# A two-layer graph kernel: 50 tiles of one class and 9 tiles of mixed classes in place of 73 padded tiles

## The reference, cut to what matters

```python
feat = concat([x[src], x[dst]], axis=1)            # 8192 x 2048
e = relu(feat[kind] @ W_kind + b_kind)             # 3 kinds: 128 hh, 640 oo, 7424 ho edges
logit = (e @ W_a + b_a)[:, 0]
alpha = softmax of logit over the edges with the same dst
z = segment_sum(alpha * x[src], dst)
new = relu(concat([x, z]) @ W_hn or W_on + b)      # nodes 0..63 and 64..255
x1 = layernorm(x + new)
```

## Time and profile before

| | us |
|---|---|
| median of three runs | 349.36 |
| span of the profiled execution, first to last instruction | 345.9 |
| what the median has beyond that span (start and end of an execution) | 3.5 |
| tile loop: first to last reduction on DVE | 142.3 to 229.2 |

### The profile page before, as it was taken

The page is one execution under the profiler, slowest core; times in us unless marked ns, Lnnn a source line. Parts: engine busy times, 40 slices in busy tenths (PEclk is TensorE's granted clock), DMA queues, the critical chain, the costliest instruction groups (busy, mean ns, idle before and its releaser), DMA issues.

```text
span 345.9 us, 4739 instructions
## 1 busy us (share of the span) xinstructions
PE 325.6 (94%) x1496; PEld 250.8 (73%) x1496; DVE 290.3 (84%) x415; ACT 195.6 (57%) x306; POOL 116.4 (34%) x128
## 2 busy tenths in 40 slices
PE   7899999999999999999999999999899999979980
PEld 7678887677644788588888888888686676758730
DVE  0999999973999979899999999988888877894545
ACT  3755396202043346588888888737149576821355
POOL 4200061084000840079999999720001200060000
PEclk9999999999999999999999999999999999999996
DMA  6999599789999996003030000023498886000003
GB/s 225 402 406 408 235 310 389 246 264 235 300 363 286 375 372 217 0 0 123 3 121 2 0 3 1 2 61 123 169 350 290 321 328 243 2 0 1 0 0 121
DMA packets 17654, 63.10 MB, mean 182 GB/s; under 512 B 2250, under 2 KB 2252, under 8 KB 17376
## 3 DMA queue, kind: packets, MB, share of 16 engines
q1 hardware_dynamic: 13536, 50.07, 39.1%
q0 software_dynamic: 2096, 8.74, 8.7%
q10 hardware_dynamic: 2000, 4.00, 3.5%
HBM read 59.64 MB, written 3.16 MB: 182 GB/s over the span
## 4 chain that ended last, share of the span: by engine, by line
DVE 45%; PE 43%; ACT 5%; DMA 2%; issue 2%; SPq 0%; ACTq 0%; DVEq 0%
DVE ps L1033 25%; PE ps L1227 12%; PE ps L1276 8%; DVE W_lo L796 5%; PE ps L1434 5%; PE ps L1505 4%; PE ps L1246 3%; DVE lo_in_raw L796 3%; PE ps L1442 2%; DMA W_raw<-in_L_gnn_W_oo_dram 2%; PE ps L1537 2%; PE ps L1469 2%; DVE tile_val L815 1%; PE ps L1308 1%; PE ps L1290 1%
## 5 line engine op out<-in xcount | busy, mean ns | idle before, releaser
L505 ACT CAST W_hi<-W_raw 128x1024 fp32r<-128x1024 f32 x62 | 63.0, 1045 | 58.6 <-DMA W_raw<-in_L_gnn_W_ho_dram 28.4
L1033 DVE SCALAR_TENSOR_TENSOR ps<-ps,wa_bc 128x1024 f32<-128x1024 f32 x73 | 86.4, 1261 | 1.3 <-PE ps L1392 1.3
L796 DVE TENSOR_TENSOR W_lo<-W_raw,W_hi 128x1024 fp32r<-128x1024 f32 x54 | 65.1, 1238 | 10.3 <-ACT W_hi L505 8.3
L1392 PE MATMUL ps<-A_tab,oh 128*128 x146 | 52.1, 438 | 0.8 <-DVE ps L1033 0.8
L1227 PE MATMUL ps<-W_hi,xT_hi 128*128 128x512 f32 x112 | 45.9, 410 | 1.0 <-DVE W_lo L796 0.9
L1392 PE MATMUL ps<-B_tab,oh 128*128 x146 | 45.9, 395 | 0.0
L1227 PE MATMUL ps<-W_lo,xT_hi 128*128 128x512 f32 x112 | 43.7, 390 | 0.0
L1227 PE MATMUL ps<-W_hi,xT_lo 128*128 128x512 f32 x112 | 34.6, 390 | 0.0
L454 POOL TENSOR_SCALAR sc<-sc 128x256 f32<-128x256 f32 x37 | 32.6, 882 | 3.2
L452 POOL TENSOR_TENSOR sc<-irow,keys 128x256 f32<-128x256 f32 x37 | 23.7, 641 | 26.5 <-PE ps L1399 26.0
L1392 PEld LDWEIGHTS ps<-B_tab,oh 128*128 128x128 f32 x146 | 27.4, 188 | 6.2 <-issue 0.5
(11 more groups left out here) (283 smaller groups left out, 585.4 us busy)
## 6 DMA issues: line engine op xcount, KB each, us to landing
W_raw<-in_L_gnn_W_ho_dram SPq DMA_DIRECT2D x8, 1024.0 KB, 5.2
W_raw<-in_L_gnn_W_hh_dram SPq DMA_DIRECT2D x8, 1024.0 KB, 8.6
W_raw<-in_L_gnn_W_hn_dram SPq DMA_DIRECT2D x8, 1024.0 KB, 4.8
W_raw<-in_L_gnn_W_on_dram SPq DMA_DIRECT2D x8, 1024.0 KB, 5.2
W_raw<-in_L_gnn_W_oo_dram SPq DMA_DIRECT2D x7, 1024.0 KB, 12.2
W_raw<-in_L_gnn_W_dram SPq DMA_DIRECT2D x4, 1024.0 KB, 4.9
key_rows<-key_rows_scratch POOLq DMA_DIRECT2D x1, 2304.0 KB, 13.8
table_scratch<-tabs ACTq DMA_DIRECT2D x2, 1024.0 KB, 6.4
```

The costliest lines, as they stand in the source:

```text
L505: sa.copy(halves(n)[0], W_raw[:, n // 2 % NS, n % 2, :]).then_inc(hi_made, 1)
L796: v.tensor_tensor(lo, W_raw[:, n // 2 % NS, n % 2, :], hi.bitcast(F32), ALU.subtract).then_inc(lo_made, 1)
L1033: v.scalar_tensor_tensor(acc, acc, 0.0, wa_bc[:], ALU.max, ALU.mult, accum_out=keys[:, t, 2:3]).then_inc(reduced, 1)
L1392: ins = mm(acc[:, n * 512:(n + 1) * 512], oh[:, t // 2 % 2, k, t % 2 * P:(t % 2 + 1) * P], tab[:].rearrange("p q d -> p (q d)")[:, n * 512 ...
```

## The change

- NL is 50 tiles of one class, and NM = 9 further tiles hold the left-over edges of any class. A class gets its full tiles, and the classes with the largest remainders get one more until 50 are given out; what is over goes to the mixed tiles. The slot computation on DVE grows for that. The one-hots of tiles are 60 wide (NT = 50 + 9 + 1) in place of 74.
- The ho tables are also written to DRAM: ACT copies G1 to SBUF and issues the DMAs (A rows before hoB, B rows around the end of hoB). PE waits for the A copy before hoB begins.
- For each mixed tile POOL issues an indirect fetch (source rows) and an indirect add (target rows) into one of four SBUF buffers and makes two one-hots of 128x256; DVE reduces the buffer from SBUF before tile AHEAD[r]; ACT makes two 128x256 operands; PE adds the counts (4 matmuls) and, 6 tiles later, the logits (2 fp32 matmuls of 256 columns) into bank 2.
- Bank 2 is taken by the mixed logits, so the loop's tiles share banks 3 to 7: one or both halves of a tile now wait for tile t-2 (reduced >= t-1) where all waited for t-3.
- The low halves of chunks 56 and 57 move from POOL to DVE, after "maxima" and after "P"; their high halves (ACT) move behind the last scale_ends.

```diff
+NL = 50
+NM = 9
+NT = NL + NM + 1
-NG = 3
+AHEAD = (14, 17, 20, 23, 26, 29, 32, 35, 38)
+MLAG = 6
+MB = 4
+FIRST = (4, 6, 3, 5, 3, 6)
+SOONER = (1, None, 0, 0, None, 1)
...
-            return END["hoB"] <= n < UX
+            return END["hoB"] <= n < UX - 2
...
+            def fetch_mixed(r):
+                if r >= MB:
+                    pool.wait_ge(mixed_reduced, r - MB + 1)
+                pool.indirect_dma_start(mixed_rows[r % MB], None, ho_dram[0],
+                                        bass.IndirectOffsetOnAxis(mixed_idx[:, 0, r:r + 1], 0)) \
+                    .then_inc(mixed_src_in[r % MB], 16)
+            def add_mixed(r):
+                pool.wait_ge(mixed_src_in[r % MB], 16 * (r // MB + 1))
+                pool.indirect_dma_start(mixed_rows[r % MB], None, ho_dram[1],
+                                        bass.IndirectOffsetOnAxis(mixed_idx[:, 1, r:r + 1], 0), compute_op=ALU.add) \
+                    .then_inc(mixed_in[r % MB], 16)
+            def mixed_onehots(r):
+                for k in range(2):
+                    ga.tensor_scalar(mixed_oh[:, r, k, :], irow[:, 1:N + 1], mixed_key[:, k, r:r + 1], None, ALU.is_equal) \
+                      .then_inc(mixed_oh_made, 1)
...
-            for t in range(0, NT, 2):
+            pool.wait_ge(dve_step, dve_at("hoA_b"))
+            pool.wait_ge(ho_out[0], 16)
+            fetch_mixed(0)
+            fetch_mixed(1)
+            for t in range(0, U, 2):
                 ends(t)
-                if t % 6 == 2 and 8 <= t <= 62:
-                    lows(END["hoB"] + t // 6 - 1, END["hoB"] + t // 6)
+            pool.wait_ge(scattered, 1 + JO)
+            for r in range(NM):
+                mixed_onehots(r)
+            ends(8)
+            pool.wait_ge(ho_out[1], 16)
+            pool.wait_ge(ho_out[2], 16)
+            add_mixed(0)
+            ends(10)
+            add_mixed(1)
+            ends(12)
+            fetch_mixed(2)
...
+            add_mixed(8)
+            ends(36)
+            lows(END["hoB"], END["hoB"] + 1)
+            ends(38)
+            lows(END["hoB"] + 1, END["hoB"] + 2)
+            for t in range(40, NL, 2):
+                ends(t)
+                lows(END["hoB"] + t // 2 - 18, END["hoB"] + t // 2 - 17)
+            lows(END["hoB"] + 7, UX - 2)
...
+            def target_rows(h):
+                sa.copy(bias_bc[:, h, :], G1[:, h * D:(h + 1) * D]).then_inc(act_step, 1)
+                act.wait_ge(act_step, act_at(f"B_rows{h}"))
+                act.dma_start(ho_dram[1][h * P:(h + 1) * P, :], bias_bc[:, h, :]).then_inc(ho_out[1 + h], 16)
+            def mixed_ends(r):
+                act.wait_ge(mixed_oh_made, 2 * r + 2)
+                if r >= 2:
+                    act.wait_ge(mixed_scattered, r - 1)
+                sa.copy(mixed_ops[r % 2][:, 1, :], mixed_oh[:, r, 1, :]).then_inc(mixed_made, 1)
+                act.wait_ge(mixed_reduced, r + 1)
+                sa.activation(mixed_ops[r % 2][:, 0, :], mixed_oh[:, r, 0, :], ACT.Copy, scale=mixed_logit[:, r:r + 1]) \
+                  .then_inc(mixed_made, 1)
...
+            act.wait_ge(mixed_scattered, NM)
+            take(S_log, 2, 2)
+            for t in range(NL - 4, NL):
                 scale_ends(t)
+            high(UX - 2)
+            high(UX - 1)
...
+            link(v.tensor_tensor(cum[:], cum[:], first.unsqueeze(2).broadcast_to([P, NC, JH]), ALU.add))
+            link(v.tensor_tensor(over[:], cum[:], limit.unsqueeze(2).broadcast_to([P, NC, JH]), ALU.is_ge))
+            low(8)
+            link(v.tensor_tensor(over[:], over[:], shift_by.unsqueeze(2).broadcast_to([P, NC, JH]), ALU.mult))
+            link(v.tensor_tensor(cum[:], cum[:], over[:], ALU.add))
+            low(9)
             link(v.tensor_tensor(cum[:], cum[:], cls_oh[:], ALU.mult))
-            low(7)
...
+            def reduce_mixed(r):
+                row = mixed_rows[r % MB]
+                dve.wait_ge(mixed_in[r % MB], 16 * (r // MB + 1))
+                v.scalar_tensor_tensor(row, row, 0.0, wa_bc[:], ALU.max, ALU.mult,
+                                       accum_out=mixed_logit[:, r:r + 1]).then_inc(mixed_reduced, 1)
             for t in range(NL):
+                if t in AHEAD:
+                    reduce_mixed(AHEAD.index(t))
                 reduce_tile(t)
...
+            low(UX - 2)
...
             def gather(t, sq, dq):
                 pe.wait_ge(oh_made, t // 2 + 1)
-                if t >= NG:
-                    pe.wait_ge(reduced, max(t - NG + 1, 2))
+                if t in (1, 2):
+                    pe.wait_ge(act_step, act_at(f"B_rows{t - 1}"))
+                for n in ((1, 0) if sooner(t) else (0, 1)):
+                    if t >= 3:
+                        pe.wait_ge(reduced, t - 2 if n == sooner(t) else t - 1)
...
+                if t in AHEAD:
+                    count_mixed(AHEAD.index(t))
+                if t - MLAG in AHEAD:
+                    scatter_mixed(AHEAD.index(t - MLAG))
```

211 lines of the change are left out of this document (153 added, 58 removed), and 1 row of the table DVE_STAGES.

## The result

The changed kernel takes 358.98 us (median of 4 runs, 356.98 to 367.36), the kernel before it, on the same chip, 349.34 (4 runs). The ratio is 1.0265, 95% interval 1.0228 to 1.0302: slower. Forecast were 354.0 us, in a range from 346.5 to 361.5. The profiled execution took 358.51 us, with a span of 356.6: 10.7 us more than the span before.

What follows compares the result with a forecast made beforehand. The prediction took the loop as bound by DVE, with PE and POOL close behind, and POOL as its bound after the change. Terms +3.0 +0.7 -1.8 +2.7 = +4.6 gave span 350.5, time 354.0 us, range 346.5 to 361.5.

Steps and rivals of the forecast that it cites:

- Part 1: Sort on DVE ahead of the loop: 5.5 us more work makes PE stand still 3.6 us; +3.0 us net.
- Part 2: Writing the tables to DRAM: a copy and DMA issue on ACT delay the last B casts; +0.7 us.
- the hold: In the loop, mixed reductions with two SBUF operands prolong POOL's operations: nine at 0.7 us, 6.3 us.
- Part 3: Tile loop: POOL's queue ends it at 84.7 us after the first reduction; -1.8 us where DVE alone promises 16.5.
- The signs that the prediction named: Loop: POOL over 95% busy, ACT waiting for POOL's ends from tile 28, PE for ACT's one-hots, last ends after last reduction.
- a sign of being wrong: End of the loop: the forecast would be wrong if the last reduction is what that end waits for.
- literal reading: Loop: shared SBUF port as an exclusive lock, 9 x 1.18 = 10.6 us in place of 6.3, total 4.3 us later.
- (b): Loop: indirect DMAs at median issue times, 7.2 us more on POOL, or landings at 8.3 us; time 361 us, chance 0.18.
- Part 4: Behind the loop: ACT's high halves delay the counts' copy 2.0 us, low(56) 0.2, low(57) 0.5; +2.7 us.
- (a): Loop: POOL keeps up, port costs little, loop ends with DVE and PE at 78.3 us; time 347.2 us, chance 0.24.
- (c): Loop: mixed matmuls fit PE's gaps, DVE is seamless and POOL cheap; time 339 us, chance 0.04.
- (d): Sort's addition is hidden and POOL mild: within 1 us of no change, chance 0.06.

Runs made afterwards that it cites:

- b3: Kernel before the change, with six more operations in DVE's sort ahead of low(10) (three small, three of 128x928, no effect on results): 353.83 us, ratio 1.0128.
- e4: Changed kernel with ACT's copy of B's first rows behind the last B casts instead of ahead of them: 360.56 us, ratio 1.0314.
- e1: Changed kernel with low(10) put ahead of the first tile conversions on DVE: 358.51 us, ratio 1.0295.
- b1: Kernel before the change, with nine more 128x1024 operations on DVE in the tile loop, each reading two SBUF operands: 362.65 us, ratio 1.0395.
- b2: Kernel before the change, with nine more 128x1024 operations on DVE in the tile loop, each reading one operand from PSUM: 360.43 us, ratio 1.0313.
- e7: Changed kernel with the low halves of chunks 52 to 55 moved from POOL to DVE: 358.43 us, ratio 1.0254.
- e5: Changed kernel without the 14 indirect fetches and adds of mixed tiles 2 to 8, whose reductions reuse the first two buffers: 354.7 us, ratio 1.0146.

## Why the prediction was right in its mechanism, and where its size was off

The time lay inside the range, 5.0 us above the point, and the direction was as forecast. Point by point:

**Part 1 (forecast +3.0 at the loop).** The stall before chunk 10 was 4.36 us, not 3.6: low(10) came 6.1 later, not 5.5: behind low(6) DVE's timeline has 16 short operations, not 15, and the two on 256 numbers take 0.45 each, not 0.36. b3 showed that such a debt goes one to one to the first reduction. Not foreseen was TensorE's clock at 0.50 behind the stall, which added 1.5 us by the first perm. The 0.8 us back from narrower sorting matmuls were 0.34 (in the chain, from the first perm to the group of 40 matmuls behind the hh edges: 32.33 us before, 31.99 after). Together this part cost 5.4 us in place of 3.0.

**Part 2 (forecast +0.7).** The rest of the delay up to the first reduction is 1.5 us. Some 0.6 of it is DVE held beside POOL's one-hots: the second L1123 took 0.60, where the first, not held, took 0.42, and the operations of 512 columns around it took up to 0.17 more than theirs before. The other 0.9 the prediction would give to the copy and the DMA issue ahead of the last B casts, which began at 145.99. e4 took them out and got 0.2 to 0.4 back, since DVE was as late. So the copy's share is not shown to be 0.7, and the hold was missing.

**Part 3 (forecast -1.8, measured -0.6).** This was the heart of the forecast, and it held in the changed kernel: POOL's queue from ends(8), 6.6 us after the first reduction (6.7 forecast), runs with no pause over 0.3 us to the last ends at 86.1 (84.7 forecast). The signs that the prediction named came in part. ACT waits for POOL's ends (1.70 and 3.28 us) only at the last tiles, not from tile 28 on; PE waits for ACT's one-hots for 1.1 us in all; POOL is busy 91% of the loop, not over 95. And e1, with the same loop, shows the last reduction ending it, which was to be a sign of being wrong: the two paths are too close for the forecast to choose between them. Adds cost 1.60 and 0.16 in place of 1.53 and 0.30, fetches 1.04 and 0.16 in place of 0.94 and 0.30: right. The hold was the term mis-sized, 7.6 in place of 6.3; b1 against b2 gives 0.86 for one, in place of 0.7. The prediction's literal reading of the Trainium skill, 10.6 us, took a whole DVE operation for each; nine times what is left of one fits. DVE waited 3.0 us for add 4, issued at 185.53 and there at 191.95, 6.4 us later; the prediction had waits for landings only in rival (b), at a landing of 8.3. The estimate of 3.2 us from the Trainium skill, "DMA: Bandwidth & Descriptors", section "Anatomy of one DMA — SWDGE (gpsimd) path", by which no reduction would wait, does not hold in this loop. e1 and e7 show the second path, level with POOL's.

**Part 4 (forecast +2.7, measured +4.6).** The copy of the counts came 0.9 later, not 2.0, since ACT's DMA issues and high halves ran beside the last scatters and not after them. Low(56) cost 0.23 and low(57) 0.65, as forecast. Two things were missed: L1130 held behind POOL's last low halves (+1.1), although the forecast itself had the rows of such a hold and applied them only to POOL, and the clock at chunk 57 (+1.75), behind PE's waits of 2.56 us for the softmax and 0.66 for low(57).

**The rivals.** (a) POOL keeps up: refuted by the chain of waits, though e5 shows what it would have given, 5 us in the loop. (b) came nearer in time (361) than the forecast's point. Of its two halves, the issues were as cheap as taken; the landings that DVE or the chain waited for took 6.0 to 7.4 us, under its 8.3, and held DVE rather than POOL's queue. (c) falls with DVE and PE alone at 81.2. (d) falls with b3.

**Where the sum failed.** The span grew by 10.7 us, the sum had 4.6. Of the 6.1 between, 3.3 are TensorE's clock behind two waits (1.5 behind chunk 10, 1.75 at chunk 57), 3.0 the hold between DVE and POOL (0.6 ahead of the loop, 1.3 in POOL's loop, 1.1 at L1130), and the rest are small terms of both signs. The clock's share is read from the slower matmuls; no run here shows the kernel without it. So two steps failed by size or omission, and neither is the choice of the bound: in part 1 and part 4 a stall of PE was priced at its length, though slower matmuls come behind it; and the hold was priced on POOL alone and for the mixed reductions alone. The clock fell once more within the loop, to a mean of 0.68 from 195 to 200 us, behind the wait for add 4; what that costs there is not separated from POOL's path, which runs beside it; in e1, where the chain runs over it, it is some 2.9 us.

One term of the sum is not what it was taken for. The 3.5 us that the median was to have beyond the span are 1.7 to 2.2 in nearly every execution of the record. The other 1.5 lie in the choice of the execution: the kernel before has spans of 345.7 to 346.0 us in some executions and 346.9 to 347.6 in nearly all others, and the profiled one was of the shorter kind. Its 60 matmuls late in layer 1 took 14.01 us, as in the changed kernel's profile (13.99); in b1 and b2 they took 15.6, with a clock of 0.57 at their start (b1, 323 to 326 us). So the two profiled spans differ by 10.7 us where the medians differ by 9.2 (358.51 and 349.34).

## What to carry to other kernels

Taking tiles from an engine is worth only the distance to the next one: here 14 tiles less for DVE and PE gave 0.6 us, because POOL, with 19.09 of 20 us busy before, got the DMAs. When a reduction's operand moves from PSUM to SBUF, count the hold in both directions and for every pair of operations that may meet, in the tail as well. And where PE was busy without a break, look whether slower matmuls come behind a new stall, and add them; b3 suggests that a delay of DVE in small pieces, with the clock kept, is cheaper than one in a single piece.
